# Four edits of the order of work in a four-layer graph kernel on one core: z ahead of the weights' low parts and a 257-column weights' product, shifts one tile ahead at the first layer's end, the last layer's totals in PSUM, and its third T moved

## The reference

```python
def _L0_gnn_ref(x, ...):               # attention over all nodes
    a = (x @ Wq.T + bq) @ (x @ Wk.T + bk).T * scale + adj + adj
    return softmax(a) @ (x @ Wv.T + bv)

def _L1_gnn_ref(x, ...):               # two gated sums over the neighbours
    e = where(adj != 0, exp(-leaky_relu(s_left[:, None] + s_right[None, :])), 0)
    x_a = e / (sum(e) + 1e-5) @ (x @ W_sa)
    x_b = adj @ (x @ W_gcnb) + b_gcnb
    return sigmoid(attn_a * x_a + attn_b * x_b)

def _L2_gnn_ref(x, ...):               # mean over the neighbours
    return (adj != 0) @ (x @ W + b) / deg

def _L3_gnn_ref(x, ...):               # attention over the neighbours only
    h = x @ W3
    att = softmax(where(S > 0, h @ U @ h.T, -inf)); S = adj + eye
    return (S * att) @ h
```

## Time and profile before

| what | us |
|---|---|
| median of 3 runs | 404.36 (404.33 to 408.68) |
| the profiled execution | 405.73 |
| its span | 403.9 |
| TensorE busy | 388.6 |
| VectorE busy | 339.2 |
| ScalarE busy | 252.7 |
| GpSimd busy | 118.9 |

### The profile page before, as it was taken

How to read it: one execution, slowest core, us unless ns; L and a number is a source line. 1 busy time by engine, 2 the same in 40 slices (tenths; PEclk the granted TensorE clock), 3 DMA queues, 4 the chain that set the end, 5 groups by cost and what they waited for, 6 DMA issues and landing times. The chain is left out here.

```text
span 403.9 us, 7765 instructions
## 1 busy us (share of the span) xinstructions
PE 388.6 (96%) x2651; PEld 357.7 (89%) x2651; DVE 339.2 (84%) x772; ACT 252.7 (63%) x529; POOL 118.9 (29%) x131
## 2 busy tenths in 40 slices
PE   8999999999799999999999989999999899999894
PEld 6788888999699899999899989999888789989794
DVE  4898899899786757999999989765897889699894
ACT  2554699888677576787588794245332366357772
POOL 1290000001010243332023011051010398469982
PEclk9999999999989999999999999999999999999988
DMA  8994000000000001000000000000000000010011
GB/s 254 376 379 142 0 0 2 2 0 2 0 2 0 2 1 54 2 1 2 3 0 2 2 2 2 0 2 0 2 2 0 0 2 2 0 54 1 2 53 35
DMA packets 10319, 13.98 MB, mean 35 GB/s; under 512 B 661, under 2 KB 7209, under 8 KB 10281
## 3 DMA queue, kind: packets, MB, share of 16 engines
q1 hardware_dynamic: 9736, 12.96, 9.4%
q10 hardware_dynamic: 544, 0.52, 0.4%
HBM read 12.10 MB, written 1.39 MB: 33 GB/s over the span
## 5 line engine op out<-in xcount | busy, mean ns | idle before, releaser
L1602 PE MATMUL ps<-v_hi,p_hi 128*128 128x258 f32 (+3 forms) x242 | 64.7, 298 | 1.5 <-DVE s_sb L1207 1.2
L391 POOL TENSOR_TENSOR mr_all<-mr_all,mhalf 128x4 f32<-128x4 f32 (+1 forms) x12 | 13.1, 1089 | 167.8 <-DVE mr_all L888 167.8
L1603 PE MATMUL ps<-v_lo,p_hi 128*128 128x258 f32 (+3 forms) x242 | 61.4, 283 | 0.0
L1602 PEld LDWEIGHTS ps<-v_hi,p_hi 128*128 128x128 f32 (+3 forms) x242 | 45.1, 186 | 3.3 <-issue 1.8
L1603 PEld LDWEIGHTS ps<-v_lo,p_hi 128*128 128x128 f32 (+3 forms) x242 | 45.1, 186 | 0.6
L1607 PE MATMUL ps<-v_hi,p_lo 128*128 128x258 f32 (+3 forms) x242 | 40.5, 286 | 1.1 <-DVE p_lo L1171 1.1
L974 DVE TENSOR_TENSOR s_sb<-s_sb,ps 128x512 f32<-128x512 f32 (+3 forms) x63 | 38.4, 610 | 0.8 <-PE ps L1589 0.7
L428 POOL TENSOR_TENSOR mid_lo<-adjT_sb,mid_hi 128x512 fp32r<-128x512 f32 (+2 forms) x16 | 20.1, 1258 | 51.0 <-ACT mid_hi L663 51.0
L1607 PEld LDWEIGHTS ps<-v_hi,p_lo 128*128 128x128 f32 (+3 forms) x242 | 32.8, 186 | 1.8 <-DVE p_lo L1171 1.6
L1894 PE MATMUL ps<-big_hi,p_lo 128*128 128x256 f32 (+3 forms) x121 | 32.7, 299 | 0.6 <-ACT p_lo L848 0.5
L1602 PE MATMUL ps<-big_hi,mid_hi 128*128 128x258 f32 (+3 forms) x121 | 31.7, 293 | 0.0
(11 more groups left out here) (251 smaller groups left out, 1230.8 us busy)
## 6 DMA issues: line engine op xcount, KB each, us to landing
adjT_sb<-in_adjT_dram SPq DMA_DIRECT2D x1, 2816.0 KB, 16.5
adjT_sb<-in_adjT_dram SPq DMA_DIRECT2D x3, 768.0 KB, 9.1
adjT_sb<-in_adjT_dram SPq DMA_DIRECT2D x1, 1815.0 KB, 20.9
out_dram<-x_sb SPq DMA_DIRECT2D x10, 128.0 KB
x_sb<-in_x_dram SPq DMA_DIRECT2D x2, 256.0 KB, 3.5
x_sb<-in_x_dram SPq DMA_DIRECT2D x1, 512.0 KB, 3.7
adjT_sb<-in_adjT_dram SPq DMA_DIRECT2D x1, 512.0 KB, 11.4
rows_sb<-in_rows_dram SPq DMA_DIRECT2D x1, 385.0 KB, 11.4
```

What stands on the lines that cost most here:

```text
L1602: pe.matmul(out_ap, left_[0][0:k, n % RING, mine], right_[0][0:k, j, 0:cols_], start=(j == 0), stop=False)
L1603: pe.matmul(out_ap, left_[0][0:k, n % RING, mine], right_[1][0:k, j, 0:cols_], start=False, stop=False)
```

## The change

- **Start.** VectorE makes z before it takes either low part of wa. The weights' product gets a 257th column: the key bias, copied by ScalarE behind the key weights, so that the product with the query weights gives Wq^T bk, and the separate `weight_column(6, ...)` and an idle product go. ScalarE copies the new column out twice. TensorE transposes all four z right behind that product. VectorE takes wb_lo after two of the four new statistics and aggregates (L883 before) between the two halves of T's low part. TensorE does values(0) ahead of score(0).
- **First layer's end.** From step 32 on VectorE shifts one tile further ahead; the last maximum is reduced at step 33 between weights_lo and shift.
- **Second layer.** `join` stands ahead of `adj_lo`; the five `mask_2` of steps 14 to 18 go to steps 9, 10 and 15 to 17.
- **Last layer.** The third T is made at step 11, between the transposing and the spreading of group 0's maximum, in banks 0 and 3; ScalarE's w_hi(0) moves ahead of values(10). GpSimd makes all 33 weights; its adds for tiles 19, 20, 21 follow the weights of tiles 22, 23, 24. Of the last group's totals VectorE adds eight tiles in PSUM bank 7 (`last_totals`) and GpSimd three (27, 29, 31); VectorE joins both (`join_totals`) before TensorE adds over the rows. Blocks 9 and 10 share bank 5.

```diff
+def late_shifts(s):
+    if s < NT - 1:
+        return range(0)
+    return range(s - 13 if s == NT - 1 else s - 12, min(s - 11, NT))
...
-SUMS3 = [[(0, 0), (0, D), (1, 0), (1, D)]] * 2 + [[(4, 0), (5, 0), (7, 0)]]
-TOTALS_BANK, COPY_BANK = 2, 3
-OWN_W = [n for n in range(2 * NB, NT) if n % 3 != 2]
+SUMS3 = [[(0, 0), (0, D), (1, 0), (1, D)]] * 2 + [[(4, 0), (5, 0), (5, D)]]
+TOTALS_BANK, COPY_BANK, LAST_TOTAL_BANK = 2, 3, 7
+POOL_TOTALS = [2 * NB + 5, 2 * NB + 7, 2 * NB + 9]
...
-T3_BANKS = [[0, 1], [6, 7], [6, 7]]
+T3_BANKS = [[0, 1], [6, 7], [0, 3]]
...
+        wq_sb = staged(11)
+        wk_sb = s_sb[:, 12:14, :].rearrange("p k n -> p (k n)")[:, 0:C * (D + 1)].rearrange("p (c n) -> p c n", c=C)
...
+            def add_last_total(n):
+
+                k = POOL_TOTALS.index(n)
+                pool.wait_ge(pf[1], n + 1)
+                pool.wait_ge(tot_add, 2 * NB - 3 + k)
+                r = totals[0][0:rows(n % NB), 0:CW[2]]
+                if k == 1:
+                    pool.wait_ge(tot_mm, 1)
+                pool.tensor_tensor(r, r if k > 1 else slot3(POOL_TOTALS[0]), slot3(n), ALU.add).then_inc(tot_add, 1)
+
...
+                weights3(n)
+                if n < 2 * NB - 3:
+                    add_total(n)
+                elif 2 * NB <= n < 2 * NB + 3:
+                    add_total(n - 3)
+                elif n in POOL_TOTALS[1:]:
+                    add_last_total(n)
...
-            act.dma_start(wk_sb, wk.rearrange("(c p) n -> p c n", p=P)).then_inc(w_in, 16)
+            act.dma_start(wk_sb[:, :, 0:D], wk.rearrange("(c p) n -> p c n", p=P)).then_inc(w_in, 16)
+            act.wait_ge(cols_in, 16)
+            act.activation(wk_sb[:, :, D:D + 1], bk_col.unsqueeze(2), ACT.Copy).then_inc(col_set, 1)
             for m in range(C):
                 act.wait_ge(gq_mm, m + 1)
-                split(0, wa_hi[:, m, 0:D], ps[:, 7 - 4 * m, m * D:(m + 1) * D], HALF_SCALE)
+                ins = act.activation(raw_b[:, m, D:D + 1], ps[:, 7 - 4 * m, D:D + 1], ACT.Copy, scale=HALF_SCALE)
+                if m == C - 1:
+                    ins.then_inc(col_set, 1)
+                split(0, wa_hi[:, m, 0:D], ps[:, 7 - 4 * m, 0:D], HALF_SCALE)
...
+            t_hi_part(2, 1)
             values(8, 1)
-            for n in range(NT):
+            exp3(0)
+            values(9, 1)
+            exp3(1)
+            act.wait_ge(t_lo[1], 2 * NG)
+            w_hi(0)
+            values(10, 1)
+            for n in range(2, NT):
                 exp3(n)
-                if n < 2:
-                    values(n + 9, 1)
-                if n:
-                    w_hi(n - 1)
+                w_hi(n - 1)
...
-            dve.wait_ge(gq_mm, 1)
-            split_lo(0, wa_lo[:, 0, 0:D], ps[:, 7, 0:D], wa_hi[:, 0, 0:D], HALF_SCALE, 1)
...
-            split_lo(0, wa_lo[:, 1, 0:D], ps[:, 3, D:2 * D], wa_hi[:, 1, 0:D], HALF_SCALE, 2)
+            for m in range(C):
+                split_lo(0, wa_lo[:, m, 0:D], ps[:, 7 - 4 * m, 0:D], wa_hi[:, m, 0:D], HALF_SCALE, m + 1)
...
-            dve.wait_ge(col_mm, 2)
-            dve.wait_ge(wv_in, 16)
-            dve.tensor_scalar(raw_b[:, :, D:D + 1], ps[:, 6, 0:C].unsqueeze(2), HALF_SCALE, None,
-                              ALU.mult).then_inc(col_set, 1)
-            first_stats(1)
-            t_lo_part(0, 0)
+            dve.wait_ge(x_in[1], 16)
+            stats(4, 0)
+            stats(5, 0)
             split_lo(1, wb_lo[:, :, :], raw_b[:, :, :], wb_hi[:, :, :])
+            stats(6, 0)
+            stats(7, 0)
+            t_lo_part(0, 0, (0,))
+            for b in blocks(1):
+                aggr(b, 0)
+            t_lo_part(0, 0, (1,))
...
-                for gi in range(NG):
+                for gi in range(2):
                     if s == NB * gi + 12:
                         top(gi, 0, ALU.max)
-                late = s >= NT - 2
-                if late:
+                if s >= NT - 1:
                     weights_lo(s - 14)
-                    if s < NT + 13:
-                        shift(s - 13, 0)
+                if s == NT:
+                    top(2, 0, ALU.max)
+                for n in late_shifts(s):
+                    shift(n, 0)
                 if s < NT:
                     add(s)
                 if s == 14:
                     weights_lo(0)
-                if not late and s >= 13:
+                if 13 <= s < NT - 1:
                     shift(s - 13, 0)
-                if 14 < s < NT - 2:
+                if 14 < s < NT - 1:
...
-                if k + 1 < NT and (k + 1) % 2 == 0:
-                    adj_lo(k + 1)
                 for gi in range(2):
                     if k == NB * gi + 19:
                         join(gi)
+                if k + 1 < NT and (k + 1) % 2 == 0:
+                    adj_lo(k + 1)
...
-                if 14 <= k < 19:
-                    mask_2(k - 14)
+                if 9 <= k < 11:
+                    mask_2(k - 9)
+                if 15 <= k < 18:
+                    mask_2(k - 13)
...
+            def last_totals(n):
+
+                j, r = n - 2 * NB, ps[0:rows(n % NB), LAST_TOTAL_BANK, 0:CW[2]]
                 dve.wait_ge(pf[1], n + 1)
-                dve.wait_ge(phi, NT + n - 2)
-                dve.wait_ge(w_copied, n - 2)
-                dve.tensor_tensor(full3(n), slot3(n), adj_tile(n), ALU.mult).then_inc(w_own, 1)
+                if j == 0:
+                    dve.tensor_copy(r, slot3(n)).then_inc(last_total, 1)
+                else:
+                    dve.wait_ge(last_total, j - sum(k < n for k in POOL_TOTALS))
+                    dve.tensor_tensor(r, r, slot3(n), ALU.add).then_inc(last_total, 1)
+
+            def join_totals():
+
+                dve.wait_ge(last_total, NB - len(POOL_TOTALS))
+                dve.wait_ge(tot_add, 2 * NB)
+                dve.tensor_tensor(totals[0][:, 0:CW[2]], ps[:, LAST_TOTAL_BANK, 0:CW[2]], totals[0][:, 0:CW[2]], ALU.add).then_inc(last_total, 1)
...
-                for n in tiles_at(s, 1):
-                    if n in OWN_W:
-                        times_s(n)
                 for n in tiles_at(s, 2):
                     weights3_lo(n)
+                for n in tiles_at(s, 1):
+                    if n >= 2 * NB and n not in POOL_TOTALS:
+                        last_totals(n)
...
+            join_totals()
...
+            pe.wait_ge(col_set, 1)
             for m in range(C):
-                weight_product(7 - 4 * m, wq_sb, wk_sb, [m]).then_inc(gq_mm, 1)
+                for c in range(C):
+                    ins = pe.matmul(ps[:, 7 - 4 * m, 0:D + 1], wq_sb[:, c, m * P:(m + 1) * P], wk_sb[:, c, :], start=(c == 0),
+                                    stop=(c == C - 1))
+                ins.then_inc(gq_mm, 1)
...
+            pe.wait_ge(ident_in, 16)
+            for b in range(4):
+                turn(b, 0)
             pe.wait_ge(cols_in, 16)
             pe.wait_ge(prep_v, 1)
             weight_column(5, wk_sb, bq_col)
-            pe.wait_ge(ident_in, 16)
-            turn(0, 0)
-            turn(1, 0)
             for c in range(C):
                 ins = pe.matmul(ps[:, 5, C:C + 1], bq_rep[:, c, :], bk_col[:, c:c + 1],
                                 start=(c == 0), stop=(c == C - 1))
             ins.then_inc(col_mm, 1)
-            turn(2, 0)
-            turn(3, 0)
-            idle(6, 1)
-            weight_column(6, wq_sb, bk_col).then_inc(col_mm, 1)
             pe.wait_ge(wlo[0], 2)
+            pe.wait_ge(col_set, 2)
...
-                score(s, 0)
                 if s == 0:
                     pe.wait_ge(wlo[1], 1)
-                    pe.wait_ge(col_set, 1)
-                values(s, 0)
+                    values(0, 0)
+                score(s, 0)
+                if s:
+                    values(s, 0)
                 if s == 6:
                     make_t(1, 0)
                 if s == 9:
...
-                    if gi < 2 and j == 0 and b % 2 == 0:
-                        wait(pe, x_add[3], b - PER + 2)
+                    paired = b != 2 * PER
+                    if paired and j == 0 and b % 2 == (gi == 2):
+                        if gi == 1:
+                            pe.wait_ge(x_add[3], b - PER + 2)
                         pe.matmul(ps[:, SUMS3[gi][b % PER][0], :], g[0][0:1, 0, 0:P], spare_mask[0:1, :], start=True, stop=False)
                     mine = slice((b % PER) * P, (b % PER) * P + rows(b))
...
-                for b in blocks(gi):
+                for b in (8, 10, 9) if gi == 2 else blocks(gi):
...
-                pe.wait_ge(tot_add, 10 * (gi + 1))
+                if gi < 2:
+                    pe.wait_ge(tot_add, 10 * (gi + 1))
+                else:
+                    pe.wait_ge(last_total, NB - len(POOL_TOTALS) + 1)
...
-                if s == 9:
+                if s == 11:
+                    pe.wait_ge(t_lo[1], 2 * C)
+                    turn_max(0, 1)
                     make_t(2, 1)
-                if s == 11:
-                    pe.wait_ge(t_lo[1], 2 * NG)
```

(36 more changed lines are left out.)

14 lines of the change are left out of this document (3 added, 11 removed).

## The result

| | us |
|---|---|
| before, median of 20 runs | 405.61 |
| changed, median of 20 runs | 403.56 (402.92 to 405.16) |
| ratio | 0.9942, 95% interval 0.9919 to 0.9966 |
| the changed kernel's profiled execution, its span | 404.91, 403.1 |

The account below looks back on a forecast made before the run. TensorE, busy 388.6 of 403.9 us, was taken as the bound, leaving only its gaps and slow-clock stretches. Terms -0.7 - 2.6 - 1.4 - 1.0 + 2.1 = -3.6 us, from 404.36 to 400.8; range 398 to 403, chance 0.64.

Parts of the forecast that it names:

- start: Kernel start: z of four blocks begins earlier, so the first T and the next transpose come earlier; -0.7 us.
- first layer's end: Shifts one tile ahead remove TensorE's 1.30 us gap and the half clock behind it, less a later maximum; -2.6 us.
- second layer: Join ahead of mask and low part removes TensorE's 1.16 us wait, and 0.2 more from the results' pace; -1.4 us.
- third T: Last layer: third T fills the 0.43 us wait at the first maximum, and the first sum waits less; -1.0 us.
- last totals: Last layer's end: TensorE waits 3.7 us for GpSimd's deferred adds, partly offset by less VectorE stretching; +2.1 us.
- My own sign of being wrong: No 3 to 4 us wait, half clock for over 4 us, or TensorE waits on VectorE's low parts in the middle.
- rival (3): Last layer: clock stays half for all eleven tiles after the 3.7 us gap; whole +3.8, 408.2 us; chance 0.06.
- (1), the end wins: Last totals: deferred adds cost nothing and stretching all comes back; end -3.4, in all -9.1, 395.3 us; chance 0.10.
- (2), the middle gives back: Nearly full VectorE loses second layer, third T and half of first layer's end; +0.1, some 404.4 us; chance 0.20.

Follow-up runs that it names:

- e1: Changed kernel with TensorE's row sum of group 1 behind tile 25's sum, VectorE's reciprocal and output adds four steps later: median 399.32 us, lowest 398.46.
- e6: Kernel before with only the last-totals edit (weights on GpSimd, adds deferred, last totals in PSUM): median 409.88 us, ratio 1.0123.
- e10: Changed kernel with seven idle products in TensorE's wait before the row sum of group 1: median 401.68 us, ratio 0.9908.
- e3: Changed kernel with the last-totals edit taken back, the four other edits kept: median 400.90 us, lowest 399.30.
- e2: Changed kernel with GpSimd adding tiles 19, 20 and 21 each behind its own weights again: median 399.51 us, lowest 399.31.
- e5: e1 with the second layer's join and masks in their old places: median 399.60 us, lowest 399.26.
- e7: e1 with the whole start as in the kernel before: median 399.89 us, lowest 399.32.
- e8: e1 with the last layer's third T and first w_hi in their old places: median 399.38 us, lowest 399.05.
- e9: Changed kernel, adds of tiles 19 to 21 behind their own weights, row sum of group 1 behind tile 25's sum: median 399.43 us, lowest 398.97.
- e11: Changed kernel, adds of tiles 19, 20, 21 behind weights of 22, 24, 26, row sum behind tile 27's sum: median 398.08 us, lowest 397.95.

## Why the prediction was right or wrong

| term | forecast | in the two profiles | undone in a run (lowest) |
|---|---|---|---|
| start | -0.7 | -0.9 | -0.9 |
| first layer's end | -2.6 | -3.8 | -3.5 |
| second layer | -1.4 | -0.7 | -0.8 |
| third T | -1.0 | -0.5 | -0.6 |
| half clock at 350 | 0 | +1.3 | |
| last totals | +2.1 | +3.8 | +4.5 |
| sum | -3.6 | -0.8 | |

The last cell is the changed kernel's lowest against e1's, 402.92 less 398.46, which compares the wait and its clock with an end that has neither. The profile of the kernel before had half clock of its own at the first layer's end and in the last group.

**Right: which waits go and which one comes.** Above all the wait: I gave 3.7 us in front of the group-1 row sum for GpSimd's third deferred add, and it is 3.62; the walk through GpSimd's queue gave its end to 0.2 us (385.05 less the 4.6 won before it is 380.43, and it is 380.28). The first four terms sum to -5.9 where I had -5.7, but by errors that cancel.

**Wrong: the clock behind that wait.** The step that failed is "From there the eleven tiles took 14.4 us, to 398.08, with half clock in part. I keep that clock." The kernel before had 3.3 us of half clock there, behind waits of under 0.5 us; behind 3.62 us it is 6.7. At 0.50 instead of 0.53 this loses 3.35 us of TensorE's work instead of 1.55, 1.8 more, and the term is short by 1.7. In the profiles it shows as tile 22 0.7 later than I had it (the row sum at half clock) and as 1.0 more from there to the last row sum, 0.9 of it on tiles 22 and 23. Tile 22's first product was at 383.72 before, and tile 24's at:

```profile
387.35 0.28 PE L1894 MATMUL ps<-big_hi,p_lo 128*128 128x256 f32 x1
```

In the changed kernel the two are:

```profile
382.06 0.56 PE L1936 MATMUL ps<-big_hi,p_lo 128*128 128x256 f32 x1
...
387.03 0.28 PE L1936 MATMUL ps<-big_hi,p_lo 128*128 128x256 f32 x1
```

That is 3.63 us for tiles 22 and 23 before and 4.97 now, 0.45 of it the opening product that I had added; behind them the error is 0.1. My own sign of being wrong, half clock for over 4 us, is there with 6.7. (The 399.75 that I called a low product of the last tile is the time of the last row sum, for the 14.4 us run to that; the sum isn't touched.)

Nor was my base a fair one. The 400.8 started from a median of three, 404.36, where twenty give 405.61. And the lowest executions of the kernel before have a mean clock of 0.998, so next to no half clock, while none of the changed kernel's 20 is over 0.990. The long wait seems to make certain what was occasional before. That fits the end costing 4.7 alone in the medians, though 3.8 between two profiles that both had a dip there; e6's profile has a further stretch below full clock, 0.91 from 354 to 372. e10 shows that the clock is a cause of its own, worth 1.9 us. What the Trainium skill says ("TensorE: Matmul & The Clock Gate", What's actually happening), that idleness throttles the array, agrees with the 0.50 behind the 3.62 us, and I used it for rival (3) alone, not for the size of the term. Rival (3) was thus true at its start, but in the profile the clock came back after 6.7 us, not never.

**First layer's end: 2.6 was too small.** I charged 0.6 for the later maximum; it was turned only 0.2 later relative to the first one (wait 0.42, now 0.61). And the waits ahead of line 1521 summed to more than the one of 1.30: between the two points 47 us and 106.7 TensorE gained 2.4, where I had 1.1. The clock gave 1.35 more, where I had 1.6.

**Second layer and third T: half of it.** The 1.16 us wait fell to 0.16, as foreseen, and by the third layer 0.3 of this was given back. I had added 0.2 for the pace of the join's results and got nothing for it: the four take 1.66 us as before. At the third T the first sum's wait fell by 0.39 and the maximum's by 0.43, but 0.44 us of wait came at the turning (0.20 before, 0.64 now), since VectorE reaches the maximum no sooner: the wait moved from the spread to the turn.

**The rivals.** (1), the end wins: no. Even with the wait taken out (e1) the end is worth nothing by the sum of the four parts and 0.8 at most by the lowest times against e3, and with the adds spread 0.5 more, where the rival had 3.4. The seven stretched products are gone, 6.5 us, but eight totals of 0.5, a join and GpSimd's seven more weights came. The exclusive lock of the Trainium skill ("SBUF — State Buffer", SBUF: two separate sides) may well explain the 936 ns, but no run here isolates it. Taking these products away from VectorE was not enough to win. (2), the middle gives back: no, -5.9 stands at the row sum of group 0. (3) is told above.

**Not foreseen: half clock at 349.5.** In the profile it costs 1.3 (-5.9 becomes -4.6). In e1 and e2 the same TensorE order, with the same 0.15 to 0.18 us of idleness in the stretch before, had a clock of 1.00 there. The clock was full there in e5, e7, e8 and e10 too. It was 0.66 from 349 to 354 in e3, e9 and e11. What decides it isn't shown. It is a second term that the prediction put at nothing, and at 1.3 us not much smaller than the first.

## What to carry to other kernels

When work is deferred on one engine, look at who waits for its last piece and move that consumer by as much: here the deferral did no harm by itself, and one row sum that kept its place in TensorE's queue turned it into a loss of over 4 us. Price a TensorE wait with the clock behind it: a dip behind short waits is no measure of one behind a long wait. And look at what paces the work there: 3.4 us of half clock cost 0.1 us in one place and over 1 us in others. Where a wait can't be moved, idle products in it may pay.

## What the hardware showed that I had not expected

The longer wait had the longer half clock behind it: 1.30 us of standing was followed by 3.4 us of it, and 3.62 us by 6.7 (granted 0.50); two waits of under 0.5 us were also followed by 3.3. Short idleness gave a dip in some executions and none in others with the same order of work there: at 110 in the profile of the kernel before, none from 110 to 116 in e6 with the same order there; from 12 to 15.5 us at the start in e8 (0.51, first row below), none in e1; and at 350. What such a dip of 3.4 us costs hangs on the place: 1.3 us at 349.5 between the two profiles, 1.4 at 110, about 1.2 at the start in e8 (400.33 against 399.14 for an execution at 0.997), 0.1 in e2 at 380. Most of these are more than the start, the join with the masks, or the third T is worth, so single executions of this kernel can't tell parts of under a microsecond apart unless their mean clock is the same.

```profile
12.00:15.50 3.50, 3.50 (x10) 0.51 1.05 389
```

```profile
384.80:392.00 7.20, 7.19 (x31) 0.53 0.05 18
```

The second row is e6 behind its wait of 3.61 us, the same as in the changed kernel. And a mask of the second layer (1.52 us in the earlier trace rows) takes 0.42 us (183.24) where the change put one, with GpSimd idle:

```profile
183.24 0.42 DVE L1250 TENSOR_SCALAR spare_mask<-adjT_sb 128x512 fp32r<-128x512 f32 x1
```
